# Where the variance of the last recurrent layer is computed, and which engine sums the squared GELU features

## The reference

```python
x = x + xcond(layernorm(x))          # part 1
x = x + ffn(layernorm(x))            # part 2

# xcond: 4 layers, run forward and backward over the tokens
z       = sigmoid(h @ Wz.T + bz)
h_tilde = tanh(h @ Wh.T + bh)        # Wz = Wh and bz = bh here
h_new   = linear_scan(clip(1 - z), z * h_tilde)
if i > 0: h_new = h_new + h
h       = (h_new - mean) * rsqrt(var + 1e-5) * gamma + beta
# then concat(h_fwd, h_bwd) @ fusion_W.T + fusion_b

# ffn: W_fc 2048 x 512 and W_proj 512 x 2048, both rounded to -1, 0, 1
h = gelu(x @ q(W_fc).T)
h = (h - mean) * rsqrt(var + 1e-5) * ln_w + ln_b
out = h @ q(W_proj).T
```

## Time and profile before

| | us |
|---|---|
| median of three runs | 1541.29 |
| the profiled execution | 1541.36 |
| its span in the profile | 1539.5 |
| PE busy | 1519.3 (99%) |
| DVE busy | 1337.0 (87%) |
| ACT busy | 1022.7 (66%) |
| POOL busy | 1010.9 (66%) |

### The profile page before, as it was taken

How to read it: one execution, slowest core, us unless ns; L and a number is a source line. 1 busy time by engine, 2 the same in 40 slices (tenths; PEclk the granted TensorE clock), 3 DMA queues, 4 the chain that set the end, 5 groups by cost and what they waited for, 6 DMA issues and landing times.

```text
span 1539.5 us, 22931 instructions
## 1 busy us (share of the span) xinstructions
PE 1519.3 (99%) x7744; PEld 1203.2 (78%) x7744; DVE 1337.0 (87%) x1893; ACT 1022.7 (66%) x1688; POOL 1010.9 (66%) x1141
## 2 busy tenths in 40 slices
PE   9999999999999999999999999999999999999999
PEld 7887888888888888888888877777777777777776
DVE  8998999999899989999888888786878888787877
ACT  7988789898687897787987444445444444444354
POOL 6766657578868678676788655565665666565566
PEclk9999999999999999999999999999999999999999
DMA  4211212321312112122044541030202020111001
GB/s 171 76 38 67 105 54 90 123 70 63 124 41 83 58 39 90 68 90 89 29 146 143 195 167 42 1 110 0 91 20 89 21 89 22 62 48 41 29 15 41
DMA packets 73157, 113.20 MB, mean 74 GB/s; under 512 B 5193, under 2 KB 37961, under 8 KB 69970
## 3 DMA queue, kind: packets, MB, share of 16 engines
q1 hardware_dynamic: 72754, 111.21, 21.2%
q10 hardware_dynamic: 288, 0.52, 0.1%
HBM read 73.95 MB, written 37.77 MB: 73 GB/s over the span
## 4 chain that ended last, share of the span: by engine, by line
PE 51%; DVE 2%; ACT 1%; issue 0%; POOL 0%; DVEq 0%; ACTq 0%; POOLq 0%
PE ps L639 15%; PE ps L620 15%; PE ps L572 11%; PE ps L499 6%; PE ps L519 1%; PE ps L585 1%; PE ps L533 1%; PE ps L649 1%; PE ps L662 0%; DVE bnp L1132 0%; ACT H L876 0%; DVE yb L1112 0%; DVE H L1120 0%; ACT AH L880 0%; DVE H L1121 0%
## 5 line engine op out<-in xcount | busy, mean ns | idle before, releaser
L499 PE MATMUL ps<-AH,WH 128*128 128x512 f32 x896 | 367.0, 410 | 7.8 <-DVE H L1121 6.1
L499 PE MATMUL ps<-AL,WH 128*128 128x512 f32 x896 | 351.1, 392 | 0.0
L499 PE MATMUL ps<-AH,WL 128*128 128x512 f32 x896 | 349.4, 390 | 0.0
L1687 POOL TENSOR_TENSOR acq<-acq,sq 128x512 f32<-128x512 f32 x120 | 182.4, 1520 | 153.7 <-ACT sq L963 153.1
L1572 POOL TENSOR_TENSOR H<-H,yb 128x512 f32<-128x512 f32 x192 | 246.2, 1293 | 8.4 <-DVE yb L1112 1.3
L1112 DVE TENSOR_TENSOR_SCAN yb<-ab,ps 128x512 f32<-128x512 f32 x192 | 232.1, 1209 | 15.8 <-POOL ab L1563 9.4
L950 ACT ACTIVATE g<-ps 128x512 f32<-128x512 f32 x128 | 76.6, 598 | 250.4 <-PE ps L620 250.4
L837 ACT ACTIVATE yb<-ps,ncnd 128x512 f32<-128x512 f32 x224 | 158.5, 707 | 86.7 <-PE ps L499 83.9
L1307 DVE SCALAR_TENSOR_TENSOR gl<-g,wbcol,gh 128x512 fp32r<-128x512 f32 x118 | 125.3, 1062 | 94.3 <-ACT gh L960 93.5
L499 PEld LDWEIGHTS ps<-AH,WH 128*128 128x128 f32 x896 | 168.5, 188 | 46.7 <-DVE H L1121 8.7
L499 PEld LDWEIGHTS ps<-AL,WH 128*128 128x128 f32 x896 | 168.1, 188 | 37.1
(11 more groups left out here) (193 smaller groups left out, 3212.4 us busy)
## 6 DMA issues: line engine op xcount, KB each, us to landing
hs_scratch<-H SPq DMA_DIRECT2D x16, 1024.0 KB, 5.4
hc<-hs_scratch SPq DMA_DIRECT2D x32, 512.0 KB, 4.2
xr<-in_x SPq DMA_DIRECT2D x32, 256.0 KB, 4.4
out<-ob SPq DMA_DIRECT2D x32, 256.0 KB, 2.2
xbuf<-in_x SPq DMA_DIRECT2D x7, 1024.0 KB, 7.5
RAW<-in_wt SPq DMA_DIRECT2D x16, 256.0 KB, 6.3
stg<-in_fct SPq DMA_DIRECT2D x16, 256.0 KB, 3.1
stg<-in_pjt SPq DMA_DIRECT2D x16, 256.0 KB, 2.8
```

Source lines behind the costliest of these rows:

```text
L499: r = e.matmul(GATE[i % 3][:], w[:, q, m * 128:(m + 1) * 128], a[:, q, :], start=(n == 0), stop=(n == 11))
L1687: e.tensor_tensor(acq[b % 2][:], acq[b % 2][:], sq[:], ALU.add).then_inc(f_s2, 1)
```

## The change

The factor rl of the last layer is no longer made in the recurrent stage for batches 1 to 7. The function turned() says which tails are still transposed there: those of layers 0 to 2, and of the last layer only batch 0. For the others the FFN stage computes the variance from the states that it loads anyway, unit by unit (28 units, u = 4 to 31):

- ScalarE squares the loaded unit, hc into hsq (state_squares), 128x1024;
- GpSimd adds the four feature blocks of each direction, for the states and for the squares (state_sums): an addition of 128x512 and one of 128x256 for each, into hsum;
- TensorE transposes hsum, four blocks, into the bank TURNED (spread);
- VectorE sums the bank over its free dimension and forms mean square minus squared mean in three small instructions (factors);
- GpSimd takes the power -1/2 (state_factors), and resid(u, 0) now waits for it.

The tables squared_at, added_at and spread_at say behind which chunk each step stands. Besides, squares(j), the addition of sq to acq, moves from GpSimd's program to VectorE's, behind total(j). load_unit(u) gets two more waits, for the square and for the first sum of the unit that had the buffer before.

```diff
@@ after the table FUSE_AT
+def squared_at(b, c):
+    u = 4 * b + {1: 5, 4: 6, 7: 7, 13: 8}.get(c, 4 * NB)
+    return u if u < NU else None
+def added_at(b, c):
+    u = 4 * b + {2: 5, 5: 6, 8: 7, 14: 8}.get(c, 4 * NB)
+    return u if u < NU else None
+def spread_at(b, c):
+    u = 4 * b + {(0 if b > 0 else 1): 4, 4: 5, 7: 6, 10: 7}.get(c, 4 * NB)
+    return u if u < NU else None
...
+def turned(t):
+    return t[2] < 3 or t[0] == 0
...
@@ TensorE: tokens(); feat(); the new spread()
-            if tau is None:
+            if tau is None or not turned(TAILS[tau]):
                 return
...
+            if u >= 4:
+                e.wait_ge(f_hr, u // 4 * 4 - 4 + min(u % 4 + 2, 4))
...
+        def spread(u):
+            b, n = (u - 4) // 4, u - 4
+            e.wait_ge(f_hs, 4 * n + 4)
...
+            else:
+                e.wait_ge(f_xh, u - 1)
+                e.wait_ge(f_xl, u - 1)
+            for k in range(4):
+                r = e.transpose(TURNED[:, k * 128:(k + 1) * 128], hsum[:, k, :], ident[:])
+            r.then_inc(f_ht, 1)
...
-        tokens(LAST, 0)
-        tokens(LAST, 1)
...
             fc(j)
+            if spread_at(b, c) is not None:
+                spread(spread_at(b, c))
...
@@ ScalarE: the new state_squares()
+        def state_squares(u):
+            i, n = u % 2, u - 4
+            e.wait_ge(d_hc[i], 16 * (u // 2) + 16)
+            if n == 0:
+                e.wait_ge(d_hs[3], 64)
+            else:
+                e.wait_ge(f_hs, 4 * n - 1)
+            e.activation(hsq[:], hc[i][:], ACT.Square).then_inc(f_hq, 1)
...
+        state_squares(4)
         for j in range(NB * NC):
             b, c = j // NC, j % NC
             hidden(j)
+            if squared_at(b, c) is not None:
+                state_squares(squared_at(b, c))
...
@@ VectorE: stats() has the same early return as tokens(); the new factors(); resid(); squares() comes here
+        def factors(u):
+            n, r = u - 4, u % 2
+            e.wait_ge(f_ht, n + 1)
+            e.reduce_sum(htot[:, r, :], TURNED[:].rearrange("p (k n) -> p k n", k=4), axis=AX_X).then_inc(f_hr, 1)
+            e.wait_ge(f_hr, n + 1)
+            e.scalar_tensor_tensor(hmean[:, r, :], htot[:, r, 0:2], 1.0 / 512 ** 2, htot[:, r, 0:2], ALU.mult,
+                                   ALU.mult).then_inc(f_hm, 1)
+            e.tensor_scalar(hve[:, r, :], htot[:, r, 2:4], 1.0 / 512, EPS, ALU.mult, ALU.add).then_inc(f_he, 1)
...
+            e.tensor_tensor(hvar[:, r, :], hve[:, r, :], hmean[:, r, :], ALU.subtract).then_inc(f_hv, 1)
...
             if h == 0:
-                if t == 0:
+                if u >= 4:
+                    e.wait_ge(f_rl, u - 3)
+                elif t == 0:
...
+        def squares(j):
+            e.wait_ge(f_sq, j + 1)
...
+            e.tensor_tensor(acq[b % 2][:], acq[b % 2][:], sq[:], ALU.add).then_inc(f_s2, 1)
...
-        stats(LAST, 0)
         unit_lo(3)
-        stats(LAST, 1)
...
             low_part(j)
+            if spread_at(b, c) is not None:
+                factors(spread_at(b, c))
...
             total(j)
+            squares(j)
...
@@ GpSimd: inv() has the early return; the new state_sums() and state_factors(); squares() leaves
+        def state_sums(u, of_squares):
+            n, k = u - 4, 4 * (u - 4) + 2 * of_squares
+            src = (hsq if of_squares else hc[u % 2])[:].rearrange("p (d q) t -> p d q t", d=2)
+            pair = hpair[:].rearrange("p (d q) t -> p d q t", d=2)
...
+            e.tensor_tensor(pair, src[:, :, 0:2, :], src[:, :, 2:4, :], ALU.add).then_inc(f_hs, 1)
+            e.wait_ge(f_hs, k + 1)
+            if n > 0 and not of_squares:
+                e.wait_ge(f_ht, n)
+            e.tensor_tensor(hsum[:, 2 * of_squares:2 * of_squares + 2, :], pair[:, :, 0, :], pair[:, :, 1, :],
+                            ALU.add).then_inc(f_hs, 1)
+        def state_factors(u):
...
+            e.tensor_tensor(rl[:, u // 4, :, u % 4], hvar[:, r, :], nhalf[:, 0:2], ALU.pow).then_inc(f_rl, 1)
...
-            squares(j)
+            if spread_at(b, c) is not None:
+                state_factors(spread_at(b, c))
+            if added_at(b, c) is not None:
+                state_sums(added_at(b, c), 0)
+            if c > 0 and added_at(b, c - 1) is not None:
+                state_sums(added_at(b, c - 1), 1)
...
@@ SyncE: load_unit()
+            if u >= 6:
+                e.wait_ge(f_hq, u - 5)
+                e.wait_ge(f_hs, 4 * (u - 6) + 1)
             e.dma_start(hc[i][:], hs[b, :, :, q * 128:(q + 1) * 128]).then_inc(d_hc[i], 16)
```

More of the change, by code:

```diff
@@ L172 @@
         _i = subject(_who, _s - _o)
-        if _i is not None and _what == "T":
-            USERS += [("T", _i, _n, 0), ("T", _i, _n, 1)]
+        if _what == "T":
+            USERS += [] if _i is None or not turned(TAILS[_i]) else [("T", _i, _n, 0), ("T", _i, _n, 1)]
         elif _i is not None and (_who == "x" or TAILS[_i][2] < 3):
@@ L177 @@
 USERS += [("F", _u, _h) for _u in range(4) for _h in (0, 1)]
-USERS += [("T", LAST, _n, _i) for _n in (0, 1) for _i in (0, 1)]
 BANK = {u: n for n, u in enumerate(USERS)}
@@ L188 @@
 LOWS = {u: n + 1 for n, u in enumerate(u for u in order(START_LOW, LOW_SLOT) if layer(u) < 3)}
-STATS = {u: n + 1 for n, u in enumerate(order(START_STAT, STAT_SLOT) + [("h", LAST, 0), ("h", LAST, 1)])}
-INVS = {u: n + 1 for n, u in enumerate(order(START_INV, INV_SLOT) + [("h", LAST, 0), ("h", LAST, 1)])}
+STATS = {u: n + 1 for n, u in enumerate(u for u in order(START_STAT, STAT_SLOT) if turned(TAILS[u[1]]))}
+INVS = {u: n + 1 for n, u in enumerate(u for u in order(START_INV, INV_SLOT) if turned(TAILS[u[1]]))}
 SHIFTS = {u: n + 1 for n, u in enumerate(u for u in INVS if layer(u) < 3)}
@@ L308, in pixart_block @@
     sg = sb(p2, "sg", [128, 2, 4])
-    sb(p2, "pad", [128, 336])
+    htot = sb(p2, "htot", [128, 2, 4])
+    hmean = sb(p2, "hmean", [128, 2, 2])
+    hvar = sb(p2, "hvar", [128, 2, 2])
+    hve = sb(p2, "hve", [128, 2, 2])
+    sb(p2, "pad", [128, 304])
     x18 = sb(p2, "x18", [128, 512])
@@ L325, in pixart_block @@
     xh.append(sb(p2, "xh1", [128, KC, S], F32R))
-    glx = sb(p2, "glx", [128, 4, S], F32R)
+    with ExitStack() as p4:
+        glx = sb(p4, "glx", [128, 4, S], F32R)
+    with ExitStack() as p5:
+        hsq = sb(p5, "hsq", [128, 8, 128])
+        hpair = sb(p5, "hpair", [128, 4, 128])
+        hsum = sb(p5, "hsum", [128, 4, 128])
+    sb(p2, "under", [128, 4, S])
     gh = [sb(p2, f"gh{i}", [128, S], F32R) for i in range(3)]
@@ L390, in pixart_block @@
     f_rd = sem("f_rd")
+    f_hq, f_hs, f_ht, f_hr, f_hm, f_he, f_hv, f_rl = (
+        sem(n) for n in ("f_hq", "f_hs", "f_ht", "f_hr", "f_hm", "f_he", "f_hv", "f_rl"))
     f_ma, f_mp = sem("f_ma"), sem("f_mp")
@@ L586, in feat @@
             r.then_inc(f_t1, 1)
+        def spread(u):
+            b, n = (u - 4) // 4, u - 4
+            e.wait_ge(f_hs, 4 * n + 4)
+            if n % 4 == 0:
+                e.wait_ge(f_xh, u)
+                e.wait_ge(f_xl, u)
+            elif n % 4 == 1 and b > 0:
+                e.wait_ge(f_rd, 2 * b - 1)
+            elif n % 4 == 1:
+                e.wait_ge(f_hr, n)
+            else:
[4 more added lines that the diff above has]
+            r.then_inc(f_ht, 1)
         def fc_of_first(t):
@@ L633, in proj @@
                 e.wait_ge(f_x1, 8)
-                e.wait_ge(s_bs, 2 * STATS[("h", LAST, 1)])
             for t in range(4):
@@ L1117, in scan @@
                 e.wait_ge(d_hs[s + 1], stored((b - 2, 1, 3)))
-                e.wait_ge(s_t1, max(T1N[("T", TAIL[(b - 2, i, 3)], p, 1)] for i in (0, 1) for p in (0, 1)) + 1)
+                if b == 2:
+                    e.wait_ge(s_t1, max(T1N[("T", TAIL[(0, i, 3)], p, 1)] for i in (0, 1) for p in (0, 1)) + 1)
             e.tensor_tensor_scan(H[s][:, m, :], ab[c][:], GATE[c][:], 0.0, ALU.mult, ALU.add).then_inc(s_sf, 1)
@@ L1321, in total @@
             e.tensor_tensor(acc[b % 2][:], acc[b % 2][:], g[j % 2][:], ALU.add).then_inc(f_s1, 1)
+        def squares(j):
+            b, c = j // NC, j % NC
+            e.wait_ge(f_sq, j + 1)
+            if c == 0:
+                if b >= 2:
+                    e.wait_ge(f_st, 2 * b - 2)
+                if j == 0:
+                    e.wait_ge(s_sc, 4 * NJ)
+                e.tensor_copy(acq[b % 2][:], sq[:]).then_inc(f_s2, 1)
+                return
+            e.wait_ge(f_s2, j)
+            e.tensor_tensor(acq[b % 2][:], acq[b % 2][:], sq[:], ALU.add).then_inc(f_s2, 1)
         def columns():
@@ L1668, in addx @@
             e.tensor_tensor(xr[i][:], xr[i][:], fbb[:], ALU.add).then_inc(f_xf, 1)
+        def state_sums(u, of_squares):
+            n, k = u - 4, 4 * (u - 4) + 2 * of_squares
+            src = (hsq if of_squares else hc[u % 2])[:].rearrange("p (d q) t -> p d q t", d=2)
+            pair = hpair[:].rearrange("p (d q) t -> p d q t", d=2)
+            if of_squares:
+                e.wait_ge(f_hq, n + 1)
+            else:
```

(25 more changed lines are left out.)

8 lines of the change are left out of this document (added).

## The result

The change makes the kernel slower: 1566.85 us (1565.57 to 1570.52, four runs) against 1541.30 of the kernel before, a ratio of 1.0169 with a 95% interval of [1.0156, 1.0181]. That is 25.5 us more; I had forecast 1549.0 and a range of 1533 to 1560. The profiled execution took 1566.32 us, its span is 1564.3, 24.8 more than before.

The account below looks back on a forecast made before the run. TensorE was taken to bound both stages, with VectorE close behind in the recurrent one. From 1541.36: - 22.6 recurrent stage, + 12.3 spreads, + 14.4 load wait, + 2.0 VectorE, + 1.5 start gives 1549.0 us, range 1533 to 1560.

Parts of the forecast that it names:

- the load's wait: Chunk 5, batches 1 to 6: ScalarE's square waits for its load, TensorE idles 2.4 us at fuse, 14.4 in all.
- The chunk-8 term: Ahead of resid in chunk 8: VectorE gets 1.9 us more against 2.1 in hand; 0.3 a batch, bounds 0 and 1.5.
- VectorE's added work: FFN stage: squares and factors don't make VectorE the bound but shrink its margins before resid; 2 us in all.
- Rival 3: VectorE late at every fuse, its squares ahead of resid each perhaps meeting a state sum: 1563 us, chance 0.09.
- the term that decides: FFN stage: the wait of ScalarE's square for the load of unit 4b + 6, 14.4 us over six batches.
- Rivals 1 and 2: Load's wait hidden, 1534.6 us, chance 0.22; or half of it or less left, 1539.4 to 1542, chance 0.14.
- The recurrent stage: 52 groups of last-layer transposes removed give back 22.6 us, bounds 17 and 27.6; VectorE can't become late there.
- Rival 4: Recurrent stage: gates and scans set the slots, half of the 22.6 us is lost: 1560 us, chance 0.05.
- The signs for the batches: Period of batches 1 to 6 grows from 83.0 by 4 to 5 us; forecast wrong if only 1.8 or above 7.
- The spreads: FFN stage: 28 spreads of four transposes on TensorE cost 0.44 us each, 12.3 us in all.
- The start: Chunks 0 to 2 of batch 0: three squares come ahead of VectorE's resid, 1.5 us paid, bounds 0 and 3.
- total: VectorE's addition in the FFN stage: its mean falls from 1.68 us to below 1.2.

Follow-up runs that it names:

- small_sums_c5: Changed kernel with GpSimd's state sums nearly empty (2 of 128 tokens from the second unit on) and the state square of unit 4b + 6 a chunk later: 1538.31 us.
- small_sums: Changed kernel with GpSimd's state sums nearly empty (2 of 128 tokens from the second unit on), the square left at chunk 4: 1561.38 us.
- late_sums: Changed kernel with GpSimd's state sums waiting for resid of their chunk, the square left in chunk 4: 1566.73 us.
- square_c5: Changed kernel with ScalarE's state square of unit 4b + 6 behind hidden of chunk 5 instead of chunk 4: 1567.17 us.
- filler9: Changed kernel with nine unused matmuls on TensorE in chunk 6 of batches 1 to 6, ahead of the fuse that waits: 1566.14 us.
- both_ways: Changed kernel with 13 of the 14 removed last-layer tails kept in the recurrent stage as well: 1585.17 us.
- late_adds_c5: Changed kernel with the square of unit 4b + 6 in chunk 5, and state sums and add_c both held behind resid: 1540.62 us.

## Why the prediction was wrong

**What failed** is two terms of about equal size. The forecast's span would have been 1547.1 us (1539.5 + 7.6), the trace's is 1564.3. Of these 17.2 us, 8.1 lie in batches 1 to 6 and 7.5 in the recurrent stage; the rest is at the start and in the spreads.

**The price of a batch.** Beside the spreads I had 2.4 us for the load's wait and 0.3, with a bound of 1.5, for chunk 8: 2.7 a batch, 16.4 in all with the seventh. The changed kernel pays 4.1 (88.95 against the 84.86 of small_sums_c5), 24.5 in six batches. Two things that I had wrong lie there side by side, and by the runs either is enough for the missing part.

- *The low clock behind an idle* was in no term: I priced a wait by its length alone. Each of the six is followed by 1.7 us lost at half the clock, which makes it cost up to 3.9 us. In small_sums and late_sums, where chunk 8 isn't late, a batch with such a stretch takes 88.7 to 89.4 us all the same.
- *The chunk-8 term* under "VectorE's added work" was too small. With the load's wait out of the way it is 1.95 us in each of six batches (square_c5). I counted 1.7 us of meetings "with the sums of chunk 8", as if GpSimd's program were spread over the chunks as it is written. It isn't: nothing held the sums of chunk 9 back, and both pairs fell together into the 5 us ahead of resid. There three instructions lost 1.1, 0.55 and 1.1 us, and the low part at 1184.55 one more, beside an addition of final (GpSimd, 1184.30 to 1185.75). In filler9, where the low clock is gone, a batch takes 88.9 us all the same. Rival 3 had this mechanism (VectorE late at a fuse through a state sum, 1563) and I gave it 0.09, since 16 meetings a batch go. The count was right and the wrong thing to count: what decides is which meetings stand ahead of a resid. In the changed kernel no wait at chunk 9 is left to see, so 1563 being near the result is not to this rival's credit.

**The load's wait** was right in place, cause, count and size: six times 2.0 to 2.2 us against 2.4. The chain ran as written: load issued at 1168.72, square begun 4.6 us later, 1.06 us long, and VectorE's four instructions. But calling it "the term that decides" was wrong. The two limits lie side by side, each hiding most of the other, so neither's removal shows its price: both give 28.5 us, each alone 5.5 and about 0. Rivals 1 and 2, with none or half of the wait, could not have given 1534.6 or 1540, since square_c5, in which TensorE waits only 0.5 us at that fuse, stays at 1567.17. The Trainium skill's figure ("DMA: Bandwidth & Descriptors", Anatomy of one DMA — SWDGE path), which it states for DMAs issued by GpSimd and by which the landing would be 3.2 us, doesn't describe this load of SyncE's: 4.6 us passed from its issue to the square that waited for it.

**The recurrent stage** gave 15.1 us where I took the whole 22.6, less than my lower bound of 17; 1.7 of the difference is a low clock in the first 15 us of that execution, below. Most of the rest, 5.8, is a wait that the removed transposes had covered, that of back for ScalarE's ntok. TensorE's waits between 0 and 850 us, of the changed kernel and then of both_ways:

```profile
PE ps L567 <- ACT ntok L904: 6.7, 10, 1.8
```

```profile
PE ps L567 <- ACT ntok L904: 1.9, 7, 0.3
```

4.8 us. The step that failed is "so it can't become late there": it looked at VectorE alone, while ScalarE's ntok was the one that came late. The bound of 17 had allowed for ScalarE, the term had not. Rival 4 was near it ("gates and scans set the slots"), with another reason and a price of 11.3 us that was too high; its sign, less than 17 us, came true. The signs for the batches did not fit any rival: they grew by 5.95 us, more than the 4 to 5 of the forecast and less than the 7 of rival 3.

**The spreads**, 0.44 each, were right: 84.86 against 83.0 is 1.9 for four. **The start** cost 3.0, 0.4 of it the first spread, where I had 1.5, with 3 as the upper bound: waits of 2.23 us for VectorE's n, 2.6 for GpSimd's first state sums and 0.5 at the fuse stand in place of the one of 1.8. **total** fell from 1.68 to 0.92 us on average, as said (below 1.2).

By the marks of the traces the sum is: - 15.1 for the tails, + 3.0 at the start with the first spread in it, + 1.4 for the three spreads of batch 0, + 11.1 for the 24 of batches 1 to 6 (84.86 less 83.0 a batch), + 24.5 for the two limits and the low clock together; that is + 24.9, and the spans differ by 24.8. The last term is where I had 14.4 + 2.0. How it divides between load, clock and meetings can't be said, since each part is enough to cover most of another. That these limits, not the new work, are the cost is shown: late_adds_c5 does all of the work and takes 1540.62. Mending the start, worth 3 us at most, was not tried.
